# Other first slot, split aggregate, row exponentials in PSUM, slots that end with the next pair's transposes, and own banks for pair 30 in the drain of a two-layer graph kernel

## The reference, cut to what matters

```python
# layer 0
qk = X @ Wqk; q, k = split(qk); v = X @ Wv
agg = einsum('bij,bjd->bid', adj, k * mask[:, :, None])
w = mask * einsum('bid,bid->bi', q, agg) / 16
x = layernorm(x + softmax(w, axis=1)[:, :, None] * v)
# layer 1
query, keyt, value = x @ Wq.T + bq, x @ Wk.T + bk, x @ Wv.T + bv
weight = adj * exp(einsum('bqd,bkd->bqk', query, keyt))
weight = weight / weight.sum(axis=2, keepdims=True)
out = layernorm(x + einsum('bqk,bkd->bqd', weight, value))
```

## Time and profile before

| | |
|---|---|
| median of 3 runs | 312.04 us (311.88 to 312.27) |
| the profiled execution | 311.97 us, span from first to last instruction 310.1 us |
| granted TensorE clock | 0.993 of full speed over the span, 1.00 in the slots |
| PE | 298.0 us busy (96%) |
| DVE | 223.6 us (72%) |
| ACT | 195.8 us (63%) |
| POOL | 143.2 us (46%) |
| HBM traffic | 31.1 MB, about 100 GB/s |

### The profile page before, as it was taken

The page is one execution under the profiler, slowest core; times in us unless marked ns, Lnnn a source line. Parts: engine busy times, 40 slices in busy tenths (PEclk is TensorE's granted clock), DMA queues, the critical chain, the costliest instruction groups (busy, mean ns, idle before and its releaser), DMA issues. The chain is left out here.

```text
span 310.1 us, 6526 instructions
## 1 busy us (share of the span) xinstructions
PE 298.0 (96%) x1900; PEld 269.3 (87%) x1900; DVE 223.6 (72%) x691; ACT 195.8 (63%) x453; POOL 143.2 (46%) x181
## 2 busy tenths in 40 slices
PE   8997999999999999999999999999999999999891
PEld 6876999999998999999998999999999999999780
DVE  2475778777778877777788777778877777788565
ACT  4354556676666666766666676666666766665761
POOL 2365554345555444455543345555443455542522
PEclk9999999999999999999999999999999999999997
DMA  6921224232434332234333222444423234210012
GB/s 231 327 71 35 85 88 116 52 113 83 118 119 119 119 91 80 80 105 119 119 119 111 83 73 90 118 119 119 119 85 83 81 107 119 85 53 36 34 36 101
DMA packets 19165, 31.26 MB, mean 101 GB/s; under 512 B 2128, under 2 KB 6608, under 8 KB 19152
## 3 DMA queue, kind: packets, MB, share of 16 engines
q1 hardware_dynamic: 19152, 31.11, 32.8%
HBM read 22.71 MB, written 8.39 MB: 100 GB/s over the span
## 5 line engine op out<-in xcount | busy, mean ns | idle before, releaser
L336 POOL TENSOR_TENSOR rstd<-var_eps,minus_half 128x4 f32<-128x4 f32 x31 | 31.5, 1018 | 138.6 <-DVE var_eps L669 124.5
L396 ACT ACTIVATE x<-x_sum,shift,rstd 128x256 f32<-128x256 f32 x62 | 34.0, 595 | 52.2 <-POOL shift L339 52.2
L748 PE MATMUL ps<-w_hi,xt_hi 128*128 128x512 f32 x128 | 61.6, 481 | 0.5 <-DVE w_lo L734 0.5
L750 PE MATMUL ps<-w_hi,xt_lo 128*128 128x512 f32 x128 | 50.4, 394 | 0.0
L749 PE MATMUL ps<-w_lo,xt_hi 128*128 128x512 f32 x128 | 50.2, 393 | 0.0
L275 POOL TENSOR_TENSOR x1b<-x,bv_all 128x512 f32<-128x512 f32 x32 | 41.5, 1297 | 4.3 <-DVE x L568 3.1
L344 POOL TENSOR_TENSOR xt_lo<-xt_raw,xt_hi 128x512 fp32r<-128x512 f32 x31 | 40.0, 1291 | 3.3 <-ACT xt_hi L390 3.3
L748 PE MATMUL ps<-wv_hi,x1t_hi 128*128 128x258 f32 x124 | 37.8, 304 | 0.0
L396 ACT ACTIVATE x<-x,shift,rstd 128x256 f32<-128x256 f32 x62 | 33.8, 595 | 3.5 <-POOL shift L287 3.5
L750 PE MATMUL ps<-wv_hi,x1t_lo 128*128 128x258 f32 x124 | 35.3, 285 | 0.0
L748 PE MATMUL ps<-x1t_hi,at_hi 128*128 128x256 f32 x124 | 35.1, 283 | 0.0
(11 more groups left out here) (121 smaller groups left out, 668.8 us busy)
## 6 DMA issues: line engine op xcount, KB each, us to landing
xt_raw<-xt_pairs SPq DMA_DIRECT2D x32, 256.0 KB, 2.7
x_raw<-x_pairs SPq DMA_DIRECT2D x32, 256.0 KB, 2.7
out_pairs<-x SPq DMA_DIRECT2D x31, 256.0 KB, 2.1
adjt<-adjt_pairs SPq DMA_DIRECT2D x32, 129.0 KB, 2.1
p<-params SPq DMA_DIRECT2D x1, 770.0 KB, 6.8
p<-params SPq DMA_DIRECT2D x1, 512.0 KB, 3.9
...
```

The source lines that it names most:

```text
L336: nc.gpsimd.tensor_tensor(rstd[r % 2][:, :, :], var_eps[:, :, :], minus_half[:, :, :], ALU.pow)\
L396: last = nc.scalar.activation(out[:, graph(g)], in_[:, graph(g)], ACT.Identity, bias=shift[r % 2][:, layer, g:g + 1], scale=rstd[r % 2][:, ...
L748: nc.tensor.matmul(out, s_hi, m_hi, start=first, stop=False)
L750: return nc.tensor.matmul(out, s_lo, m_hi, start=False, stop=last)
```

## The change

It has six parts.

1. From pair 4 on (`SPLIT = 4`) the aggregate is a split product: ACT makes `x_hi` and `adjm_hi`, POOL makes `x_lo` and `adjm_lo`, and PE runs six fp32r matmuls in place of two fp32 ones. POOL's slot gets `low_x` at its head and `low_adjm` at its end, and `mask_adj` moves ahead of `xt_lo`. ACT's slot gets `split_adjm` behind the row exponentials and `split_x` at its end.
2. The row exponentials go to PSUM, into the second 128 columns of the bank in which `w_row` lies.
3. In front of slot 0 and in it PE's list is reordered: aggregate 1 ahead of `transpose_p(0)`, `fold_biases` behind the projection of pair 1, `transpose_w(2)` behind the values of slot 0, and the transposes of pair 1 ahead of `transpose_p(2)`. On POOL `wv1_lo` goes a slot ahead, `mask_adj(3)` into slot -1, and `x1b(0)` waits for `x1t_lo(0)`. On ACT the `z` of slot 0 goes ahead of the norm of pair 1. DVE copies the biases later.
4. The transposes of pair t+1 stand at the end of slot t, not at the head of slot t+1.
5. In the drain pair 30 has its own `z_a`, `val_a`, `edge_a` and the banks 5 and 6 for scores and sum; its `attend` stands ahead of pair 31's values, and the values of pair 30 stay together.
6. DVE's `score_bias` of pair 29 goes behind `x1_sum(31)`, and DVE ends pair 30 before it weighs pair 31's edges.

```diff
+SPLIT = 4
+        x_hi = [sb(f"x_hi{i}", [128, PAIR_X], F32R) for i in range(2)]
+        x_lo = [sb(f"x_lo{i}", [128, PAIR_X], F32R) for i in range(2)]
+        adjm_hi = [sb(f"adjm_hi{i}", [128, PAIR_N], F32R) for i in range(2)]
+        adjm_lo = [sb(f"adjm_lo{i}", [128, PAIR_N], F32R) for i in range(2)]
-        sum_b_ps = ps[:, 5:7, :]
-        score_b_ps = ps[:, 5:7, 384:512]
+        sum_a_ps = ps[:, 5:7, :]
+        score_a_ps = ps[:, 5:7, 384:512]
+        def exp_row_ps(r):
+            return yv_ps(r)[0:2, 0, NODES:2 * NODES]
...
         # POOL
+            def low_adjm(u, r):
+                pool.wait_ge(adjm_hi_done, u + 1 - SPLIT)
+                nc.gpsimd.tensor_tensor(adjm_lo[r % 2][:, :], adjm[r % 2][:, :],
+                                        adjm_hi[r % 2][:, :].bitcast(F32), ALU.subtract).then_inc(adjm_lo_done, 1)
+            def low_x(u, r):
+                pool.wait_ge(x_hi_done, u + 1 - SPLIT)
+                nc.gpsimd.tensor_tensor(x_lo[r % 2][:, :], x_raw[r % 4][:, :],
+                                        x_hi[r % 2][:, :].bitcast(F32), ALU.subtract).then_inc(x_lo_done, 1)
             def slot(t, r):
+                if exists(t + 3) and r + 3 >= SPLIT:
+                    low_x(t + 3, r + 3)
...
+                if exists(t + 3) and r + 3 >= SPLIT:
+                    mask_adj(t + 3, r + 3)
...
-                if r == -1:
                     pool.wait_ge(wv1_hi_done, 1)
                     nc.gpsimd.tensor_tensor(wv1_lo[:, :, 0:DIM], wv1T, wv1_hi[:, :, 0:DIM].bitcast(F32), ALU.subtract)\
                         .then_inc(wv1_lo_done, 1)
+                if r == -1:
+                    mask_adj(3, 3)
+                    pool.wait_ge(x1t_lo_done, 1)
...
-                if exists(t + 3) and r >= 0:
-                    mask_adj(t + 3, r + 3)
+                if exists(t + 3) and r + 3 >= SPLIT:
+                    low_adjm(t + 3, r + 3)
...
         # ACT
+            def split_x(u, r):
+                act.wait_ge(x_loaded[r % 4], transfers4(u, r))
+                act.wait_ge(agg_done, u - 1)
+                nc.scalar.copy(x_hi[r % 2][:, :], x_raw[r % 4][:, :]).then_inc(x_hi_done, 1)
+            def split_adjm(u, r):
+                act.wait_ge(adjm_done, u + 1)
+                act.wait_ge(agg_done, u - 1)
+                nc.scalar.copy(adjm_hi[r % 2][:, :], adjm[r % 2][:, :]).then_inc(adjm_hi_done, 1)
...
-                    nc.scalar.activation(exp_row[:, :], w_row_ps(r + 2), ACT.Exp, bias=neg_max[:, 0:1],
+                    nc.scalar.activation(exp_row_ps(r + 2), w_row_ps(r + 2), ACT.Exp, bias=neg_max[:, 0:1],
                                          accum_out=exp_sum[:, 0:1]).then_inc(row_exp_done, 1)
+                if exists(t + 3) and r + 3 >= SPLIT:
+                    split_adjm(t + 3, r + 3)
...
+                if exists(t + 4) and r + 4 >= SPLIT:
+                    split_x(t + 4, r + 4)
...
         # DVE, drain
+                bias_scores(a)
                 dve.wait_ge(sum_done, DRAIN + 1)
                 attended(DRAIN, sum_ps)
-                bias_scores(a)
+                weigh_edges(a, edge_a)
...
                 variance(1)
-                weigh_edges(a, edge)
-                bias_scores(b)
-                weigh_edges(b, edge_b)
                 dve.wait_ge(sum_done, a + 1)
-                attended(a, sum_ps)
+                attended(a, sum_a_ps)
...
                 variance(1)
-                dve.wait_ge(last_sum_done, 1)
-                attended(b, sum_b_ps)
+                bias_scores(b)
+                weigh_edges(b, edge)
+                dve.wait_ge(sum_done, b + 1)
+                attended(b, sum_ps)
...
         # PE
             def aggregate(u, r):
-                pe.wait_ge(adjm_done, u + 1)
-                pe.wait_ge(x_loaded[r % 4], transfers4(u, r))
+                if r < SPLIT:
+                    pe.wait_ge(adjm_done, u + 1)
+                    pe.wait_ge(x_loaded[r % 4], transfers4(u, r))
+                else:
+                    pe.wait_ge(adjm_lo_done, u + 1 - SPLIT)
+                    pe.wait_ge(x_lo_done, u + 1 - SPLIT)
...
+                    else:
+                        mm = split_product(agg_ps[:, g, :], [(adjm_hi[r % 2][:, n], adjm_lo[r % 2][:, n],
+                                                              x_hi[r % 2][:, graph(g)], x_lo[r % 2][:, graph(g)])])
...
         # PE, drain
-                values(x1t_hi_a, x1t_lo_a, 1).then_inc(val_done, 1)
+                pe.wait_ge(z_copied, a + 1)
+                scores(score_a_ps, z_a, x1t_a)
                 pe.wait_ge(x1t_lo_done, b + 1)
-                pe.wait_ge(z_copied, a + 1)
                 queries(x1t_hi, x1t_lo)
-                pe.wait_ge(x2_done, DRAIN + 1)
-                scores(score_ps, z, x1t_a)
+                pe.wait_ge(edge_done, a + 1)
                 pe.wait_ge(val_copied, a + 1)
+                attend(sum_a_ps, edge_a, val_a, 0)
+                attend(sum_a_ps, edge_a, val_a, 1).then_inc(sum_done, 1)
                 pe.wait_ge(score_bias_done, a + 1)
                 values(x1t_hi, x1t_lo, 0)
                 values(x1t_hi, x1t_lo, 1).then_inc(val_done, 1)
                 pe.wait_ge(z_copied, b + 1)
                 pe.wait_ge(x1t_copied, b + 1)
-                scores(score_b_ps, z_b, x1t)
-                pe.wait_ge(edge_done, a + 1)
+                pe.wait_ge(x2_done, DRAIN + 1)
+                scores(score_ps, z, x1t)
+                pe.wait_ge(edge_done, b + 1)
+                pe.wait_ge(val_copied, b + 1)
                 attend(sum_ps, edge, val, 0)
                 attend(sum_ps, edge, val, 1).then_inc(sum_done, 1)
```

101 lines of the change are left out of this document (54 added, 47 removed).

## The result

| | before | after |
|---|---|---|
| median | 311.96 us (311.78 to 312.27) | 305.11 us (304.62 to 305.34, 4 runs) |
| ratio | | 0.9777, 95% interval [0.9760, 0.9794] |
| span of the profiled execution | 310.1 us | 303.5 us (execution 305.32 us) |

What follows compares the result with a forecast made beforehand. PE, busy throughout slots 1 to 28 at 8.95 us each, was taken as the bound. Terms: 4.4 - 0.2 + 2.4 + 0.7 = 7.3, so 312.04 - 7.3 = 304.7 us; range 303.4 to 308.3.

Steps and rivals of the forecast that it cites:

- Steady slots: Slots 1 to 28: split aggregate saves 4.4 us, period 8.95 to 8.79, less 0.2 for waits.
- scattered waits: Steady slots: 0.2 us booked as a loss, a first sign of POOL's chain having almost no slack.
- POOL's chain as the bound: First rival, steady slots: POOL's chain to adjm_lo, slack 0.08 us, sets the period; 8.91, time 307.8 us; 18%.
- rival 4: Steady slots: x_lo blocks x_sum as well as edge, period 9.65, slower at 328.5 us; 5%.
- x_lo's turn with `edge`: Steady slots: DVE's edge waits for POOL's x_lo and ends 0.3 us late, with DVE behind it.
- Six matmuls at the price of two: Rival, split aggregate: six fp32r matmuls save nothing over two fp32 ones, leaving parts 3 and 5; 308.9 us; 6%.
- The first slot: Start of the kernel: reordering gains 2.8 us, less 0.4 for one wait, net 2.4; aggregate 3 near 27.5.
- The link prices: Slot 0's chain to aggregate 3: x1t_hi 1.0, transpose_p(0) 0.3, z 0.7, p_row 0.4, transposes of pair 1 0.43 us.
- my lower bound: Slot 0: 7.2 us of PE work in its 10.33, giving 3.1 us as the most the first slot can gain.
- The 0.4 that the first split aggregate was to wait: First round: transpose_p(2) only 0.1 ahead of the aggregate, so POOL's chain has less time; about 0.4 us lost once.
- Exponentials in PSUM: p_row's source moved from SBUF: worth nothing in steady slots, since PE is never idle there.
- The drain: End of the kernel: last attend starts about 0.2 us later, x2(31) comes 0.7 us earlier, at 303.65.

Runs made afterwards that it cites:

- e1: The change with all aggregates as two fp32 matmuls again, without the casts and low parts: 308.65 us, ratio 0.9887.
- e9: The change without a hardware loop, slots 4 to 27 written out for all engines in unchanged order: 306.58 us, ratio 0.9819.
- e4: The change with a hardware loop of 12 slots run twice instead of 4 slots run six times: 308.54 us, ratio 0.9888.
- e8: The change with the last three DVE operations of a slot moved to the head of the next loop pass: 304.91 us, ratio 0.9765.
- e3: The change with POOL making x_lo only for pairs 4 and 5, later pairs using the old values: 304.98 us, ratio 0.9773.
- e7: The change with a useless 128x128 memset on POOL ahead of every adjm_lo: 306.44 us, ratio 0.9813.
- e2: The change with the row exponentials back in SBUF: 306.32 us, ratio 0.9828.
- e5: The change with the drain of the kernel before, its banks, buffers and order on PE, ACT and DVE: 306.14 us, ratio 0.9803.

## Why the prediction was right, and where its terms were off

- **Steady slots, 4.2 predicted, 3.5 measured.** The mechanism held. The six matmuls cost 0.02 to 0.03 more than booked: they save 0.14 a slot instead of 0.156 (e1, and the fifteen even slots of e9), 3.9 in place of 4.4 over 28. The booked 0.2 for scattered waits was 0.7. Of it 0.5 to 0.6 is the five slots behind a taken branch, in which DVE's `p_col` and `x_sum` are 0.1 late. That was hidden while the aggregate took 0.87, and is exposed now (e1 against the change; e4, e8, e9 for the branch). The rest is POOL's chain. Against this stand 0.28 us that part 4, booked at zero, or something else in the lists gave (see e1).
- **POOL's chain as the bound** (the first rival) happened in miniature: it binds in about half of the slots, by 0.01 to 0.05, and costs some 0.1 to 0.3 us in all (e3, e7), with a slack of 0.06 to -0.05 where 0.08 was worked out. What would have come of a longer chain was priced too high: "the period is then chain + 0.15 - 0.54" leaves out that a late aggregate also makes the next chain's time longer. With it only half of the excess is paid in a slot (e7), so 0.1 us costs 1.4 us and not 2.8, and rival 4 is too high in the same way. x_lo's turn with `edge` is as long as was said (e3).
- **Six matmuls at the price of two, and `x_lo` blocking `x_sum`**: both excluded by the rows, 0.12 and 0.88.
- **The first slot, 2.4 predicted, 2.2 measured from the span's start and 2.5 from the first projection matmul**: right as a sum, with its terms off to both sides. Measured by taking back one at a time: `z` 1.1 for 0.7, `x1t_hi` 0.4 for 1.0, `p_row` 0.5 for 0.4, the transposes 0.15 for 0.43. The front with the earlier `transpose_p(0)` gave 0.25 for 0.3, by the traces of before and after alone. The link prices were read in the order before, in which other instructions stood beside them, and that the errors cancel is luck as far as the single links go. Slot 0 is 7.20, my lower bound, but slot 1 is 9.78 instead of 8.94: `transpose_p(2)` and its wait moved into it (0.54), and the projection waits 0.31 for `x_sum`. Aggregate 3 starts at 27.79 and not near 27.5. The 0.4 that the first split aggregate was to wait isn't there, as these waits in slot 1 had made room for `adjm_lo`, which ends 0.07 behind the start of the transposes of pair 2.
- **Exponentials in PSUM**: "worth nothing" in the steady slots failed. It is right for the ordinary ones; in the first slots of a pass it saves 0.1 each, 0.5 us in all (e2). The step that failed is the inference from a PE without idle time: it holds for slots without a branch, where `p_row` may end 0.3 later for nothing, but behind a taken branch the aggregate's weight load was seen 0.94 to 0.98 behind the end of `p_row` (e2, e8), so that a later `p_row` is a later aggregate.
- **The drain, 0.7 predicted, 0.8 measured** (e5: 0.76 between attend and `x2(31)`). The last attend was to start 0.2 later and starts 0.05 earlier; from there to `x2(31)` are 1.48 and not 1.40.

The terms predicted add up to 7.3 and the medians differ by 6.9; the measured parts of the spans make 6.6, or 6.9 with the 0.3 by which the start of the profiled execution was late. What is missing from 7.3 is the 0.7 of the steady slots, of which the start and the drain give some back.
